# Two tiles in one product for q, k and up, and turned norms that pass DRAM block by block

## The chip, the cores and the metric

The kernel runs on one core of one Trainium2 chip. The metric is the device time of one execution in microseconds (us), the median of several runs. Everything is float32.

## The reference, cut to what matters

The input is 8 sequences of 2048 tokens with 256 features. A token passes an attention block and a feed-forward block, each behind a layer norm and followed by another one, with a residual sum:

```python
def layer(x):                                   # x: [8, 2048, 256]
    x = x + layernorm(attention(layernorm(x)))
    return x + layernorm(ffn(layernorm(x)))

def attention(h):                               # linear attention in chunks of 128 tokens
    q, k, v = h @ w_q.T, h @ w_k.T, h @ w_v.T
    sq, sk = elu(q) + 1, elu(k) + 1
    mem = (sq @ memory) / clip(sq @ memory_norm)
    A = (sq_chunk @ sk_chunk.T) * tril          # 128x128
    local = (A @ v_chunk + sq_chunk @ S) / clip(A.sum(-1) + sq_chunk @ z)
    S, z = S + sk_chunk.T @ v_chunk, z + sk_chunk.sum()
    return (g * mem + (1 - g) * local) @ w_o.T

def ffn(h):
    dense = silu(h @ W_up.T) @ W_down.T         # 256 -> 1024 -> 256
    # product-key routing: 4 heads, the best 8 of 1024 experts in each
    w = silu((h @ down_embed.T)[best] * softmax(scores[best]))
    return dense + sum(w * up_embed[best])
```

## The kernel before

A tile is one chunk of 128 tokens (tokens on the partitions, 256 features in a row). There are 128 tiles, taken so that the eight sequences alternate. Each engine's program is written out by hand as a loop over 142 steps: `pipeline(body)` calls `body(t, steady)`, and `t[n]` is the tile that stands at stage n in this step. In a given step `t[3]` is an early tile (its input is normed), `t[7]` is in the attention, `t[8]` has its second norm, `t[9]` and `t[10]` are in the routing and the up product, `t[12]` and `t[13]` in the two output products. All engines run free of each other and meet at semaphores alone, so the step of one engine is shifted against that of another.

**TensorE in one step**, in this order: up product of `t[10]` (L723 to L735, 16 products with 128 columns, the two halves into banks 1 and 2), q and k of `t[7]` (L752 to L756, 8 products with 128 columns), v, the expert output product of `t[13]`, the routing product of `t[9]`, the attention scores of `t[7]` (L791), the first half of the expert down product, the state and memory products, the product of masked scores and v (L817, it waits for the mask that VectorE applies at L1153), the second half of the down product, the state update (L835), the hidden output product of `t[12]` (L845). A float32 product is recorded as two weight loads and two matmuls of equal shape. All products made by `product` have line L691.

**The turned norms.** TensorE needs the two layer norms with features on the partitions: `xn1T` (first norm, used at stage 7) and `xn2T` (second norm, used by the routing and down products at stage 9 and by the up product at stage 10). They are not turned on TensorE except for the first three and the last tiles. VectorE transposes inside blocks of 32x32 (L1088, L1115) into `xn1_blocks` and `xn2_blocks`, SyncE (SP) stores the 128 KB to DRAM in one transfer of 1 KB rows (L448, L444), waits for it, and fetches it back rearranged with eight transfers of 16 KB in pieces of 128 bytes (`gather_chunks`, L437). `xn1T` and `xn2T` have two buffers each. In the step in which TensorE runs the routing product of `t[9]`, SP fetches the turned second norm of `t[8]`.

**SP's queue in one step**: store of the second norm (L444), store of the first norm (L448), store of the transposed expert weights `w_way` (512 KB, L452, it waits for VectorE's L1127), fetch of `xn2T`, store of the k features (L460), fetch of the expert weights (L430, four transfers), load of the next input (L469), fetch of the k features (L430, four), fetch of `xn1T`, store of the output (L483, it waits for VectorE's L1109). That is 30 transfers.

**GpSimd** adds the experts' weights of the heads with two accumulating transfers in each step: the pairs (1 MB, L597), then the sum of both (512 KB, L558). They run on the same 16 DMA engines as SP's transfers.

**ScalarE** takes q and k from PSUM (relu and exp, L975 and L977) and the hidden layer (silu, L947 and L892); **VectorE** makes the k and q features `sig` (L1078), the norms and the expert selection.

Of the kernel before, what the change touches and what calls it, by code (L numbers as in the profile page):

```python
# [6 lines left out]
def sandwich_kernel(nc, hidden, w_q, w_k, w_v, w_o, gate, memory, memory_norm,  # L7
# [52 lines left out]
    LATE = TILES - 2  # L60

# [7 lines left out]
    with ctx:  # L69
# [68 lines left out]
        xn1_way = nc.dram_tensor("xn1_way", [2, P, D], fp32).ap()  # L138
        xn2_blocks = sb("xn2_blocks", [P, D])
        xn2_way = nc.dram_tensor("xn2_way", [2, P, D], fp32).ap()  # L140
# [6 lines left out]
        hT = sb("hT", [P, 3, IC, P])  # L147
# [24 lines left out]
        eqk = bank[1].rearrange("p (c n) -> p c n", n=P)  # L172
# [13 lines left out]
        s_ue_cent = sem("up_embed_centred")  # L186
        s_last_ps = sem("last_weights_turned")
# [144 lines left out]

        def y_bank(t):
            return bank[{TILES - 3: 5, TILES - 2: 1, TILES - 1: 2}.get(t, 4)][:, 0:D]
# [61 lines left out]
        def _(sp):  # L396
# [36 lines left out]
            def gather_chunks(dst, way, s_in):  # L433

                for j in range(BLOCKS):
                    for c in range(DC):
                        sp.dma_start(dst[j * BLOCK:(j + 1) * BLOCK, c, :].rearrange("p (i t) -> p i t", t=BLOCK),  # L437
                                     way.rearrange("(i q) (j c t) -> j c q i t", q=BLOCK, j=BLOCKS, c=DC)[j, c]).then_inc(s_in, 16)

            def body(t, steady):  # L440
                if t[8] is not None:
                    if EARLY <= t[8] < LATE:
                        wait(sp, s_xn2_blocks_turned, t[8] + 1 - EARLY)
                        sp.dma_start(xn2_way[t[8] % 2, :, :], xn2_blocks[:, :]).then_inc(s_xn2_blocks_out[t[8] % 2], 16)  # L444
                if t[5] is not None:
                    if t[5] >= EARLY:
                        wait(sp, s_xn1_blocks_turned, t[5] + 1 - EARLY)
                        sp.dma_start(xn1_way[t[5] % 2, :, :], xn1_blocks[:, :]).then_inc(s_xn1_blocks_out[t[5] % 2], 16)  # L448
# [26 lines left out]
                if t[5] is not None:  # L475
                    if t[5] >= EARLY:
                        moved(sp, s_xn1_blocks_out, t[5], 1, TILES, EARLY)
# [768 lines left out]
```

## Time and profile before

| | us |
|---|---|
| median of 3 runs | 2849.07 (2846.18 to 2849.6) |
| the profiled execution | 2846.18 |
| span of its trace | 2844.4 |
| TensorE matmul busy | 2813.8, 99% |
| TensorE weight loads | 2268.5, 80% |
| VectorE, ScalarE, GpSimd busy | 2422.0, 2525.5, 2062.6 |
| DMA engines busy, mean of 16 | 78% |

Busy times are sums over the span, and engines work at the same time. The profiled execution was 2846.18 us, 1.8 us more than its span. Of TensorE's busy time, matmuls are pipelined and their ends are modelled, so the time that a group takes is best read from the start of the group to the start of the next one.

### The profile page before, as it was taken

Reading aid. Unit: us, or ns where it says so; the run is one execution under the profiler, and the core shown is the slowest. Engines: PE = TensorE matmul, PEld = TensorE weight load, DVE = VectorE, ACT = ScalarE, POOL = GpSimd, SP = SyncE. Lnnn points to the kernel's source line nnn. Section 1 sums busy time; section 2 is a strip of 40 time slices with the busy share of each in tenths; the row PEclk is TensorE's granted clock in tenths of the full one; section 3 lists DMA queues with packets and bytes.
Section 4 is the critical chain, followed back from the end, with each engine's and each line's share of the span. In section 5 each row is a group of like instructions: output and inputs, shape, how many; then the busy total and the mean of one; then the engine's idle time right before and its main releaser. Section 6 shows DMA issues by size and latency. Waiting matters only on the chain.

```text
span 2844.4 us, 49057 instructions
## 1 busy us (share of the span) xinstructions
PE 2813.8 (99%) x14724; PEld 2268.5 (80%) x14724; DVE 2422.0 (85%) x6125; ACT 2525.5 (89%) x3618; POOL 2062.6 (73%) x2460
## 2 busy tenths in 40 slices
PE   8899999999999999999999999999999999999999
PEld 6688788878878887888788878887887788788877
DVE  5888888888888888888888888888888888888876
ACT  5889998999898899989998999899889989998997
POOL 4677777777777777777777777777777777777774
PEclk9999999999999999999999999999999999999999
DMA  4788788778887887888778778877878888778774
GB/s 120 146 172 168 170 168 172 166 170 171 171 168 168 171 172 167 170 172 170 170 168 173 167 170 168 172 166 170 171 171 168 169 171 171 169 168 172 155 153 118
DMA packets 592909, 471.71 MB, mean 166 GB/s; under 512 B 377731, under 2 KB 527364, under 8 KB 592644
## 3 DMA queue, kind: packets, MB, share of 16 engines
q0 software_dynamic: 52832, 199.77, 40.0%
q1 hardware_dynamic: 539812, 268.81, 37.7%
q8 instruction: 117, 1.92, 0.3%
q14 instruction: 148, 1.21, 0.1%
HBM read 137.37 MB, written 131.20 MB: 94 GB/s over the span
## 4 chain that ended last, share of the span: by engine, by line
PE 94%; POOL 2%; ACT 1%; DVE 1%; issue 1%; DMA 0%; SPq 0%; POOLq 0%; DVEq 0%; ACTq 0%
PE banks L691 88%; PE banks L835 4%; PE banks L817 2%; POOL sums L539 1%; POOL rstd L525 0%; DMA wexp<-wexp 0%; POOL wexp L597 0%; ACT L1008 0%; DVE w_blocks L1127 0%; POOL cand_best L584 0%; ACT wexp L1008 0%; PE banks L626 0%; PE banks L648 0%; DVE picked L1074 0%; PE banks L668 0%
## 5 line engine op out<-in xcount | busy, mean ns | idle before, releaser
L539 POOL TENSOR_TENSOR sums<-scores 128x1024 f32<-128x1024 f32 x512 | 1005.7, 2049 | 73.9 <-ACT scores L1025 73.9
L525 POOL TENSOR_TENSOR rstd<-var_eps,minus_half 128x1 f32<-128x1 f32 x512 | 510.4, 997 | 42.0 <-ACT y_sq L935 15.5
L691 PE MATMUL banks<-deT,xn2T 128*128 128x512 f32 x1024 | 484.2, 596 | 2.5 <-DVE picked L1074 2.1
L691 PEld LDWEIGHTS banks<-xn2T,wupT 128*128 128x128 f32 x4096 | 477.2, 192 | 9.7 <-DVE state L1181 3.3
L691 PE MATMUL banks<-xn2T,wupT 128*128 128x128 f32 x4096 | 478.2, 275 | 2.5 <-DVE state L1181 2.5
L691 PE MATMUL banks<-ue,gT 128*128 128x256 f32 x2048 | 462.8, 379 | 0.0
L691 PE MATMUL banks<-wdownT,hT 128*128 128x256 f32 x2048 | 462.7, 379 | 0.0
L691 PEld LDWEIGHTS banks<-wdownT,hT 128*128 128x128 f32 x2048 | 389.1, 190 | 56.4 <-issue 2.6
L691 PEld LDWEIGHTS banks<-ue,gT 128*128 128x128 f32 x2048 | 388.8, 190 | 52.7
L577 POOL TENSOR_TENSOR wexp<-wexp,w_last 128x1 f32<-128x1 f32 x127 | 132.7, 1045 | 370.7 <-ACT z_last L1014 370.7
L691 PEld LDWEIGHTS banks<-deT,xn2T 128*128 128x128 f32 x1024 | 185.4, 191 | 135.8 <-issue 125.2
L553 POOL TENSOR_TENSOR cprob<-cmask,cdif 128x112 f32<-128x112 f32 x128 | 58.9, 460 | 271.1 <-DVE cmask L1208 271.1
L691 PE MATMUL banks<-route,xn2T 128*128 128x512 f32 x512 | 240.8, 592 | 0.8 <-ACT xn2T L882 0.8
L1074 DVE SCALAR_TENSOR_TENSOR picked<-sums,cand_best,banks 128x1024 f32<-128x1024 f32 x128 | 163.8, 1280 | 51.5 <-POOL sums L539 51.5
L1173 DVE SCALAR_TENSOR_TENSOR picked<-sums,cand_best,banks 128x1024 f32<-128x1024 f32 x128 | 163.9, 1280 | 46.3 <-PE banks L691 45.6
L1194 DVE SCALAR_TENSOR_TENSOR prob<-picked,rz,prob 128x1024 f32<-128x1024 f32 x128 | 166.2, 1298 | 36.9 <-ACT prob L939 35.4
L1082 DVE SCALAR_TENSOR_TENSOR prob<-picked,rz,prob 128x1024 f32<-128x1024 f32 x128 | 166.7, 1302 | 27.2 <-ACT prob L986 26.9
L947 ACT ACTIVATE hT<-banks 128x512 f32<-128x512 f32 x128 | 76.6, 598 | 125.2 <-PE banks L691 125.0
L1186 DVE SCALAR_TENSOR_TENSOR picked<-sums,cand_best,banks 128x1024 f32<-128x1024 f32 x128 | 163.3, 1276 | 11.6 <-POOL sums L539 11.4
L896 ACT ACTIVATE wexp<-prob 128x1024 f32<-128x1024 f32 x127 | 134.2, 1057 | 39.1 <-DVE w_blocks L1127 39.1
L961 ACT ACT_TABLE_LOAD x128 | 164.2, 1283 | 2.3
L947 ACT ACT_TABLE_LOAD x128 | 164.2, 1283 | 2.3
(162 smaller groups left out, 6649.3 us busy)
## 6 DMA issues: line engine op xcount, KB each, us to landing
wexp<-wexp POOLq DMA_DIRECT2D x127, 1024.0 KB, 8.4
wexp<-wexp POOLq DMA_DIRECT2D x127, 512.0 KB, 4.7
w_way<-w_blocks SPq DMA_DIRECT2D x127, 512.0 KB, 2.6
g_parts<-w_way SPq DMA_DIRECT2D x508, 128.0 KB, 5.6
xn_way<-xn_blocks SPq DMA_DIRECT2D x248, 128.0 KB, 1.8
x_in<-_attn_hidden_states_dram SPq DMA_DIRECT2D x128, 128.0 KB, 4.6
out_dram<-x_out SPq DMA_DIRECT2D x128, 128.0 KB, 1.8
xn1T<-xn_way SPq DMA_DIRECT2D x1000, 16.0 KB, 2.3
```

Source lines behind the costliest of these rows:

```text
L525: return nc.gpsimd.tensor_tensor(rstd[:, n, m:m + 1], var_eps[:, n, m:m + 1], minus_half[:, :], ALU.pow)
L539: return nc.gpsimd.tensor_tensor(sums[:, k, :, :], scores[:, k, 0:XIN].unsqueeze(2).broadcast_to([P, XIN, NKEYS]), scores[:, HEADS + k, :] ...
L577: nc.gpsimd.tensor_tensor(weights(t[9])[:, 0, LAST_IN:], weights(t[9])[:, 0, LAST_IN:], w_last[:, t[9] % 2:t[9] % 2 + 1], ALU.add).then_in ...
L691: last = nc.tensor.matmul(out, lhs(c), rhs(c), start=(start and c == 0), stop=(stop and c == chunks - 1))
L896: nc.scalar.activation(weights(t[10])[:, 3, :], prob[:, 3, :], ACT.Silu).then_inc(s_head_3_weights_ready, 1)
L947: nc.scalar.activation(flat(hT[:, t[9] % 3, 4:8, :]), u_ps[1][:, :], ACT.Silu).then_inc(s_hidden_1_ready, 1)
L961: nc.scalar.activation(prob[:, 3, :], head(sums, 3), ACT.Exp, bias=neg_max[:, t[9] % 2, 3:4]).then_inc(s_head_3_prob_ready, 1)
L1074: nc.vector.scalar_tensor_tensor(picked[:, 0, :], head(sums, 2), best[:, 2, TOP - 1:TOP], down, ALU.is_ge, ALU.mult).then_inc(s_head_2_sel ...
L1082: nc.vector.scalar_tensor_tensor(prob[:, 2, :], picked[:, 0, :], rz[:, t[10] % 2, 2:3], prob[:, 2, :], ALU.mult, ALU.mult).then_inc(s_head ...
L1173: nc.vector.scalar_tensor_tensor(picked[:, 0, :], head(sums, 0), best[:, 0, TOP - 1:TOP], down, ALU.is_ge, ALU.mult).then_inc(s_head_0_sel ...
L1186: nc.vector.scalar_tensor_tensor(picked[:, 1, :], head(sums, 1), best[:, 1, TOP - 1:TOP], down, ALU.is_ge, ALU.mult).then_inc(s_head_1_sel ...
L1194: nc.vector.scalar_tensor_tensor(prob[:, 1, :], picked[:, 1, :], rz[:, t[9] % 2, 1:2], prob[:, 1, :], ALU.mult, ALU.mult).then_inc(s_head_ ...
```

## The change

1. **q, k and up for two tiles at once.** From tile 12 on, q and k are made for two neighbouring tiles in one product with 256 columns: in an even step (`t[7]` even) k of tiles t and t+1, in an odd step q of tiles t+1 and t+2, always one matrix, 4 products, 512 columns of PSUM. The first q pair is made by itself in the step of tile 12, in bank 0. The up product of tiles 12 to 125 is treated the same way: the step of an even tile makes a half of the 1024 hidden units for both tiles, the next step the other half. `sig` gets a third buffer, `hT` a fourth. The up product of an even tile u now needs `xn2T` of tile u+1 at its start, and TensorE waits for it there.
2. **Turned norms.** `xn1T` and `xn2T` are laid out as [partition, chunk, tile, token] with four tiles, so that two neighbouring tiles are one row of 256. SP stores the blocks with four transfers of 32 KB in pieces of 128 bytes (`scatter`), each to its place in an already transposed array in DRAM, and fetches it back with one transfer of 128 KB in rows of 512 bytes (`turned_in`).
3. **The first norm two steps earlier.** At tiles 10 and 14 (`AHEAD`) one additional tile is normed and turned, so that from there on the input norm and `xn1T` are two stages earlier than before, since q of tile t+2 is needed in the step of tile t.

```diff
+    PAIRED = 12
+    AHEAD = (10, 14)
+    TURNED = 4
-        xn1T = sb("xn1T", [P, 2, DC, P])
-        xn2T = sb("xn2T", [P, 2, DC, P])
+        xn1T = sb("xn1T", [P, DC, TURNED, P])
+        xn2T = sb("xn2T", [P, DC, TURNED, P])
-        sig = sb("sig", [P, 2, 2 * DC, P])
+        sig = sb("sig", [P, 3, DC, 2, P])
-        xn2_way = nc.dram_tensor("xn2_way", [2, P, D], fp32).ap()
+        xn2_way = nc.dram_tensor("xn2_way", [2, D, P], fp32).ap()
...
+        def ahead(t, stage):
+
+            for lead in range(len(AHEAD) + 1):
+                u = t[stage - lead]
+                if u is not None and u not in AHEAD and len([a for a in AHEAD if a < u]) == lead:
+                    return u
+            return None
+
+        def hidden_at(t):
+            return t // 2 * 2 + 2 if paired_up(t) else t + 1
+
+        def paired_up(t):
+            return PAIRED <= t < LATE
...
+            def scatter(way, blocks, s_out):
+
+                for i in range(BLOCKS):
+                    sp.dma_start(way.rearrange("(k q) t -> q k t", q=BLOCK)[:, :, i * BLOCK:(i + 1) * BLOCK],
+                                 blocks[i * BLOCK:(i + 1) * BLOCK, :].rearrange("q (k t) -> q k t", t=BLOCK)).then_inc(s_out, 16)
+
+            def turned_in(dst, way, s_in):
+                sp.dma_start(dst, way.rearrange("(c p) n -> p c n", p=P)).then_inc(s_in, 16)
...
                     if EARLY <= t[8] < LATE:
                         wait(sp, s_xn2_blocks_turned, t[8] + 1 - EARLY)
-                        sp.dma_start(xn2_way[t[8] % 2, :, :], xn2_blocks[:, :]).then_inc(s_xn2_blocks_out[t[8] % 2], 16)
-                if t[5] is not None:
-                    if t[5] >= EARLY:
-                        wait(sp, s_xn1_blocks_turned, t[5] + 1 - EARLY)
-                        sp.dma_start(xn1_way[t[5] % 2, :, :], xn1_blocks[:, :]).then_inc(s_xn1_blocks_out[t[5] % 2], 16)
+                        scatter(xn2_way[t[8] % 2, :, :], xn2_blocks, s_xn2_blocks_out[t[8] % 2])
+                x = ahead(t, 5)
+                if x is not None:
+                    if x >= EARLY:
+                        xn1_out(x)
...
-                        moved(sp, s_xn2_blocks_out, t[8], 1, LATE, EARLY)
-                        gather_chunks(xn2T[:, t[8] % 2, :, :], xn2_way[t[8] % 2, :, :], s_xn2_blocks_in[t[8] % 2])
+                        moved(sp, s_xn2_blocks_out, t[8], BLOCKS, LATE, EARLY)
+                        wait(sp, s_up_0_in_psum, t[8] - 2)
+                        turned_in(xn2T[:, :, t[8] % TURNED, :], xn2_way[t[8] % 2, :, :], s_xn2_blocks_in[t[8] % 2])
...
+            def up(t, half):
+
+                if not paired_up(t):
...
+                else:
+                    first = t // 2 * 2 % TURNED
+                    for k in range(2):
+                        ic = 4 * (t % 2) + 2 * half + k
+                        last = product(two_tiles(u_ps[half])[:, k, :, :], DC, lambda c: wupT[:, c, ic * P:(ic + 1) * P],
+                                       lambda c: xn2T[:, c, first:first + 2, :])
+                return last
+
+            def two_tile_q_or_k(dst, w, t):
+                for ec in range(DC):
+                    last = product(two_tiles(dst)[:, ec, :, :], DC, lambda c: w[:, c, ec * P:(ec + 1) * P],
+                                   lambda c: xn1T[:, c, t % TURNED:t % TURNED + 2, :])
+                return last
...
+                    if paired_up(u) and u % 2 == 0:
+                        moved(pe, s_xn2_blocks_in, u + 1, 1, LATE, EARLY)
+                    wait(pe, s_state_ready, u + 2, KEPT)
+                    wait(pe, s_hidden_1_ready, u)
+                    up(u, 1).then_inc(s_up_1_in_psum, 1)
+                    wait(pe, s_hidden_0_ready, u)
+                    up(u, 0).then_inc(s_up_0_in_psum, 1)
...
+                    elif t[7] % 2 == 0:
+                        two_tile_q_or_k(qk_ps, wkT, t[7]).then_inc(s_qk_in_psum, 1)
+                    elif t[7] < TILES - 1:
+                        two_tile_q_or_k(qk_ps, wqT, t[7] + 1).then_inc(s_qk_in_psum, 1)
...
+                for lead, a in enumerate(AHEAD):
+                    if t[3 - lead] == a:
+                        if a - 1 <= EARLY:
+                            dve.wait_ge(s_early_ps, TURN['xn1', a - 2] + 1)
+                        dve.wait_ge(s_x_rstd, a)
+                        xn1_made(a - 1)
+                        dve.wait_ge(s_xn1_ready, a)
+                    if t[4 - lead] == a:
+                        xn1_turned(a)
```

## Rows read from the trace of the kernel before

**Rows 1.** The page, part 1: busy us, share of the span, instructions.

```profile
PE 2813.8 (99%) x14724; PEld 2268.5 (80%) x14724; DVE 2422.0 (85%) x6125; ACT 2525.5 (89%) x3618; POOL 2062.6 (73%) x2460
```

**Rows 2.** The page, part 4: the chain that ended last, shares by engine.

```profile
PE 94%; POOL 2%; ACT 1%; DVE 1%; issue 1%; DMA 0%; SPq 0%; POOLq 0%; DVEq 0%; ACTq 0%
```

**Rows 3.** Timeline of TensorE, one step: start, us, line, op, out<-in, shape, count.

```profile
1503.58 1.88 PE L691 MATMUL banks<-route,xn2T 128*128 128x512 f32 x4
...
1509.21 0.60 PE L817 MATMUL banks<-v_one,at 128*128 128x258 f32 x2
...
1512.23 3.62 PE L691 MATMUL banks<-wdownT,hT 128*128 128x256 f32 x16
1515.68 3.73 PE L691 MATMUL banks<-xn2T,wupT 128*128 128x128 f32 x32
1519.25 1.06 PE L691 MATMUL banks<-xn1T,wqT 128*128 128x128 f32 x8
...
1521.04 1.03 PE L691 MATMUL banks<-wvo,xn1T 128*128 128x256 f32 x4
...
1525.36 1.02 PE L691 MATMUL banks<-route,xn2T 128*128 128x512 f32 x2
```

**Rows 4.** Waits of TensorE: waited for, us in total, times, longest us.

```profile
PE banks L817 <- DVE at L1153: 9.2, 5, 3.5
```

**Rows 5.** Timeline of VectorE, same step; idle before and releaser in brackets.

```profile
1499.64 1.28 DVE L1074 SCALAR_TENSOR_TENSOR picked<-sums,cand_best,banks 128x1024 f32<-128x1024 f32 x1 [0.38 <-POOL sums L539]
...
1501.76 1.28 DVE L1082 SCALAR_TENSOR_TENSOR prob<-picked,rz,prob 128x1024 f32<-128x1024 f32 x1 [0.24 <-ACT prob L986]
...
1504.34 0.44 DVE L1115 STREAM_TRANSPOSE xn_blocks<-xn 128x256 f32<-128x256 f32 x1
...
1508.24 0.41 DVE L1144 BATCH_NORM_STATS2 stats<-x_in 128x6 f32<-128x256 f32 x1
...
1508.62 0.28 DVE L1153 TENSOR_TENSOR at<-banks,causal 128x128 f32<-128x128 f32 x1
1509.91 0.16 DVE L1156 TENSOR_SCALAR dens<-banks 128x2 f32<-128x2 f32 x1 [1.01 <-PE banks L817]
```

**Rows 6.** Timeline of ScalarE, same step.

```profile
1499.46 0.60 ACT L975 ACTIVATE rqk<-banks 128x512 f32<-128x512 f32 x1 [0.51 <-PE banks L691]
```

**Rows 7.** Timeline of SP's queue: start, us to issue, line, transfer, count.

```profile
1504.68 0.43 SPq L483 DMA_DIRECT2D out_dram<-x_out  x1
1505.16 0.43 SPq L444 DMA_DIRECT2D xn_way<-xn_blocks  x1
...
1507.12 0.32 SPq L452 DMA_DIRECT2D w_way<-w_blocks  x1
1507.49 4.13 SPq L437 DMA_DIRECT2D xn2T<-xn_way  x8
...
1517.60 0.74 SPq L469 DMA_DIRECT2D x_in<-_attn_hidden_states_dram  x1
```

**Rows 8.** Timeline of SP's queue at the start, a load of 256 rows.

```profile
1.71 0.43 SPq L401 DMA_DIRECT2D sums<-in_L_attn_w_q_dram  x1
```

**Rows 9.** Timeline of GpSimd, same step: the accumulating transfer of the pairs.

```profile
1510.06 1.25 POOL L597 DMA_DIRECT2D wexp<-wexp  x1
```

**Rows 10.** Line L437, transfers issued between 1507 and 1508.5 us.

```profile
L437 SPq DMA_DIRECT2D xn2T<-xn_way x2: 433/604/775, 1507.5 to 1508.0; - x2
DMA to landing us min/median/max: 2.3/2.4/2.5
```

**Rows 11.** Line L437, transfers issued between 1511 and 1511.66 us.

```profile
L437 SPq DMA_DIRECT2D xn2T<-xn_way x2: 432/432/432, 1510.7 to 1511.2; - x2
DMA to landing us min/median/max: 1.7/4.6/7.5
```

**Rows 12.** The page, part 6: transfers, KB each, median us to landing.

```profile
xn_way<-xn_blocks SPq DMA_DIRECT2D x248, 128.0 KB, 1.8
x_in<-_attn_hidden_states_dram SPq DMA_DIRECT2D x128, 128.0 KB, 4.6
```

More of the change, by code:

```diff
@@ new lines, in up @@
+            def up(t, half):
+                if not paired_up(t):
+                    for k in range(4):
+                        ic = 4 * half + k
+                        last = product(u_ps[half][:, k * P:(k + 1) * P], DC, lambda c: wupT[:, c, ic * P:(ic + 1) * P],
+                                       lambda c: xn2T[:, c, t % TURNED, :])
+                else:
[5 more added lines that the diff above has]
+                return last
@@ L718, in body @@
                         turn_wdown(0, 0)
-                    if t[10] == TILES - 3:
+                    if u == TILES - 3:
                         turn_xn('xn2', xn2, s_xn2_ready, LATE)
-                    if t[10] == TILES - 2:
+                    if u == TILES - 2:
                         turn_xn('xn2', xn2, s_xn2_ready, LATE + 1)
-                    wait(pe, s_state_ready, t[10] + 2, KEPT)
-                    for k in range(4):
-                        ic = 4 + k
-                        last = product(u_ps[1][:, k * P:(k + 1) * P], DC, lambda c: wupT[:, c, ic * P:(ic + 1) * P],
-                                       lambda c: xn2T[:, t[10] % 2, c, :])
@@ L728, in body @@
-                    last.then_inc(s_up_1_in_psum, 1)
-                    if not steady:
-                        wait(pe, s_hidden_0_ready, t[10])
-                    for k in range(4):
-                        ic = k
-                        last = product(u_ps[0][:, k * P:(k + 1) * P], DC, lambda c: wupT[:, c, ic * P:(ic + 1) * P],
-                                       lambda c: xn2T[:, t[10] % 2, c, :])
-                    last.then_inc(s_up_0_in_psum, 1)
+                    if paired_up(u) and u % 2 == 0:
+                        moved(pe, s_xn2_blocks_in, u + 1, 1, LATE, EARLY)
@@ L831, in body @@
                     if not steady:
-                        wait(pe, s_hidden_0_ready, t[8] - 1)
+                        wait(pe, s_hidden_0_ready, up_done(t[8] + 8), TILES)
                     if t[8] < KEPT:
@@ L1174, in body @@
                                                    ALU.is_ge, ALU.mult).then_inc(s_head_0_selected, 1)
-                if t[3] is not None:
-                    dve.wait_ge(s_x_stats, t[3] + 1)
-                    nc.vector.bn_aggr(mv[:, LN_X, t[3] % 2, :], stats[:, LN_X, t[3] % 2, :]).then_inc(s_x_moments, 1)
+                x = ahead(t, 3)
+                if x is not None and x - 1 not in AHEAD:
+                    x_moments(x)
                 if t[8] is not None:
@@ L1195, in body @@
                                                    ALU.mult, ALU.mult).then_inc(s_head_1_weighed, 1)
+                for lead, a in enumerate(AHEAD):
[7 more added lines that the diff above has]
+                        xn1_turned(a)
+                x = ahead(t, 3)
+                if x is not None and x - 1 in AHEAD:
+                    x_moments(x)
                 if t[7] is not None:
```

273 lines of the change are left out of this document (178 added, 95 removed).

## The prediction

> **What bounds the kernel now.** I read the page first: TensorE is busy for 99% of the span while no other engine is over 89% [rows 1], and the chain of work that ended last runs over TensorE for 94% of the span [rows 2]. Then the timeline of TensorE in one step in the middle [rows 3]: no row carries an idle time, and from the routing product of one step (1503.58) to that of the next (1525.36) there are 21.78 us. 128 such steps are 2788 us of the span of 2844.4; the other 56 us are set-up, filling and draining. TensorE's largest wait for anybody is 9.2 us in 5 places, for the mask at L1153 [rows 4]. So the middle is a pure stream of products, and an edit is worth what it takes out of that stream, as long as nobody who feeds TensorE becomes late.
>
> **Part 1, the products.** The next starts in rows 3 give the price of each shape. Sixteen instructions with 256 columns (hidden output) last from 1512.23 to 1515.68, 3.45 us, 215.6 ns each. Thirty-two with 128 columns (up) last from 1515.68 to 1519.25, 3.57 us, 111.6 ns each; the sixteen of q and k from 1519.25 to 1521.04, 1.79 us, 111.9 ns each. The change turns every two of 128 columns into one of 256. Per step 48 instructions, 5.36 us, become 24 of 215.6 ns, 5.17 us: 0.19 us less. The columns stay the same, only what an instruction costs beside its columns goes, so this is small: 3.5% of the two groups. Count: up 114 tiles x 16 = 1824 new instructions; k and q 58 pairs x 16 = 928 (the first q pair in bank 0 is among them, moved and not added); together 2752, each 223.3 - 215.6 = 7.7 ns cheaper than the two it replaces. **Sum: -21.2 us.** Bounds: the other instructions near 256 columns (L817 and its neighbours, 258 columns) follow each other in the same manner [rows 3], so I see no reason for more than 1 ns either way, 3 us in all.
>
> A rule of the Trainium skill puts this part lower. In "TensorE: Matmul & The Clock Gate", section "Wait — 56ns, not 53.3ns?", a matmul has a fixed cost of about 2.5 ns beside its columns. By that one instruction less saves 2.5 ns and the part is 2752 x 2.5 = 6.9 us; the rows show 7.7 ns, and I go by the rows.
>
> **What covers it.** The saving holds only if the others keep pace with a step of 21.59 us. VectorE: the mask ends at 1508.90 and TensorE's L817 needs it at 1509.21 [rows 3, 5], 0.31 us of slack, and this is the tightest feeder. Going back from there VectorE works without a pause to L1082, which waits 0.24 us for ScalarE [rows 5]; ScalarE in turn waits 0.51 us at L975 for the end of q and k [rows 6]. That chain starts from TensorE behind the shortened groups, so it comes earlier by the same 0.19 us. The chain that does not start there comes over GpSimd's sums into L1074 [rows 5]; it has the 0.31 and the 0.24 us, less a few hundredths for semaphores, against 0.19 needed. VectorE also waits 1.01 us for L817 in each step [rows 5]. ScalarE's and VectorE's operations keep their number and size, as q alone or k alone of two tiles is 512 columns again. Cost: nothing. Without this cover each step would lose up to 0.19 us and the part would be gone. The new waits for the hidden layer and its fourth buffer ask for things that are done a step before; nothing.
>
> **Part 2, the turned norms.** SP issues 8 stores and 2 fetches in place of 2 and 16, 22 transfers a step in place of 30, so its queue is shorter by 8 x 0.48 = 3.8 us (0.48 from L483 to L444 [rows 7]). That by itself is worth nothing, TensorE never waits for SP. What matters is that an even step's up product now needs the second norm of tile u+1 at its own start, 1515.68, where before the routing product needed it at 1525.36 [rows 3]: 9.7 us less. Before, the last piece was issued at 1511.2 and landed 7.5 us later [rows 11], at 1518.7: **under the old scheme this wait would fail by 3 us.** So the new order in SP's queue decides. VectorE has turned the norm at 1504.78 [rows 5], SP stores the output at 1504.68 and is free at 1505.16. Four stores of the second norm and four of the first, 0.48 us each, end at 1509.0; then `w_way` (it was issued at 1507.12, so 1.9 us later than before [rows 7]); then the fetch at about 1509.4. The four stores of the second norm are issued by 1507.1 and land in about 1.8 us [rows 12], at 1508.9: not late for the fetch. Behind `w_way` a fetch landed in 2.3 to 2.5 us [rows 10], so this one lands at about 1511.9, 3.8 us ahead of the up product. An issue costs 0.43 us for 256 rows too [rows 8], so I take 0.48 for the stores with 256 pieces. The edge is the pairs' accumulating transfer, issued at 1510.06 [rows 9]: of the two fetches issued at 1510.7 and 1511.2 one landed in 1.7 and one in 7.5 us [rows 11], so its data fill the engines from some 1.2 to 1.7 us after its issue, 1511.3 to 1511.8. The new fetch has its data out at about 1511.5. It is close, but a fetch cut off by half still has until 1515.68. Cost taken: nothing; bounds: 0 and the rival below. The first norm's fetch at the end of SP's step is needed two steps later as before, nothing.
>
> **Part 3, the earlier first norm.** The input is needed one step after its load: issued at 1517.60 [rows 7], landing in 4.6 us [rows 12], read at 1508.24 + 21.78 = 1530.0 [rows 5], so 7 us of slack; nothing. At the two places where a tile is slipped in, VectorE has five more operations of 0.16 to 0.44 us [rows 5], 0.8 to 2.2 us against a slack of 0.31: 0 to 1.9 us each, I take 1 us each. At the end TensorE makes the last tile's q and k, 1.79 us [rows 3], a step or two earlier; where it then waits for VectorE, that is not collected: 0 to 1.8, I take 1 us. **Sum: +3 us.**
>
> **The sum.** 2846.2 - 21.2 + 3 = 2828.0 us for an execution like the profiled one. It was 2.9 us under the median of the runs, so 2831 against 2849.07. By the bounds 2825 to 2836.
>
> **Rivals.**
> - *Late fetch, slower.* If the data of the fetch come behind those of the accumulating transfer, it lands as in rows 11: 7.5 us after 1509.4, 1516.9, up to 1518.7 where the late one landed. TensorE then stands for 1.2 to 3.0 us at L691's up product in every even step, 57 times, 68 to 171 us, middle 120: 2951. It decides from the point where eight stores take over 0.55 us each, or land after more than 3 us, or hold up the `w_way` data behind them in the same queue by 0.6 us. For it: no row shows a store of 128-byte pieces, and 512 KB of `w_way` now lie right before the fetch. Against it: the fetches in such pieces landed in 1.7 us when nothing else ran [rows 11]. Chance 0.23. The Trainium skill speaks for this rival: "DMA: Bandwidth & Descriptors", section "Specifications", says that below 512 B an engine reads, modifies and writes. No run so far shows it; if a piece cost twice as much the queue would be behind by about that much.
> - *The gain is eaten, no change.* The fetch is late by 0.4 us on average: 57 x 0.35 = 20 us, 2851. Or a 256-column instruction in these places saves only 2.5 ns (223.3 - 2.5 = 220.8 ns): 6.9 - 3 us, 2845. Chance 0.12 for both.
> - *The seams cost nothing and more is collected at the ends:* under 2825, chance 0.03. That the pairing is not done at all is excluded by the diff.
>
> **How the numbers follow.** A measurement of this kernel can tell about 0.2% from no change, that is below 2843.4 and above 2854.8. The forecast has 0.62. Faster: 0.62 + 0.03 = 0.65; same 0.12; slower 0.23. The range starts at 2823; up to 2836 it holds about 0.63, with the no-change cases 0.75, and it reaches to 2880 to take in a fetch that is late by less than 0.9 us in the even steps, which brings it to 0.8.
>
> **What would show it.** Right: up groups of 16 instructions with 256 columns and 3.45 us, a step of 21.59 us, no idle ahead of them, and the fetch of `xn2T` landing in 2 to 3 us. Wrong: idle time of TensorE ahead of the up product in every second step, put down to a transfer; mask waits of L817 in every step (then VectorE's slack was less than 0.19 us); SP's `w_way` issued after 1509.5 by this step's clock; or an up group of 3.53 us. Waits at L817 in two steps near tiles 10 and 14 would be the seams.

## The result and the profile after

The changed kernel takes 2836.33 us (median of 6 runs, 2832.46 to 2838.54); the kernel before, on the same chip, takes 2849.34 us (6 runs, 2846.18 to 2851.68). The ratio is 0.9952, with a 95% interval of 0.9941 to 0.9962: faster by 13 us. The profiled execution took 2835.43 us, its span is 2833.7 us in place of 2844.4, so 10.7 us less.

The page of the changed kernel, parts 1 and 4, then the stores of the turned norms from part 6 (out<-in, queue, count, KB each, us from issue to landing):

```profile
PE 2797.6 (99%) x11972; PEld 2176.6 (77%) x11972; DVE 2423.5 (86%) x6125; ACT 2525.7 (89%) x3618; POOL 2053.0 (72%) x2460
...
PE 85%; POOL 6%; ACT 3%; DVE 3%; issue 2%; SPq 1%; DMA 1%; DVEq 0%; POOLq 0%; ACTq 0%
...
xn_way<-xn_blocks SPq DMA_DIRECT2D x992, 32.0 KB, 1.7
```

TensorE runs 2752 products less than in [rows 1], and is still busy for 99% of the span; every other engine has the work it had. The chain of work leans on TensorE for 85% in place of the 94% of [rows 2]: the others have come nearer.

The timeline of TensorE in one step of the changed kernel, to be laid beside [rows 3]:

```profile
1501.76 1.88 PE L749 MATMUL banks<-route,xn2T 128*128 128x512 f32 x4
...
1507.39 0.60 PE L908 MATMUL banks<-v_one,at 128*128 128x258 f32 x2
...
1510.41 3.62 PE L749 MATMUL banks<-wdownT,hT 128*128 128x256 f32 x16
1513.86 3.62 PE L749 MATMUL banks<-xn2T,wupT 128*128 128x256 f32 x16
1517.32 1.89 PE L749 MATMUL banks<-xn1T,wkT 128*128 128x256 f32 x8
1519.04 1.03 PE L749 MATMUL banks<-wvo,xn1T 128*128 128x256 f32 x4
...
1523.36 1.88 PE L749 MATMUL banks<-route,xn2T 128*128 128x512 f32 x4
```

From routing product to routing product there are 21.60 us, before 21.78. The up group lasts from 1513.86 to 1517.32, 3.46 us (before 3.57); k or q from 1517.32 to 1519.04, 1.72 us (before 1.79). No row has an idle time.

**Where the 10.7 us are.** I split the span at two events that both kernels have, the starts of the 13th and of the 120th tile's routing product. The timeline of TensorE of the kernel before has them in these rows:

```profile
305.57 1.88 PE L691 MATMUL banks<-route,xn2T 128*128 128x512 f32 x4
...
2636.28 1.88 PE L691 MATMUL banks<-route,xn2T 128*128 128x512 f32 x4
```

and that of the changed kernel in these:

```profile
313.18 1.88 PE L749 MATMUL banks<-route,xn2T 128*128 128x512 f32 x4
...
2625.74 1.88 PE L749 MATMUL banks<-route,xn2T 128*128 128x512 f32 x4
```

The 107 steps between them went from 2330.7 to 2312.6 us: -18.1. The part before them became longer by 7.6 us (1.7 of it is the first q pair, which is made there ahead of its time). The part behind them went from 208.1 to 207.9 us, -0.2. Together -10.7. So the stream of products gave most of what was forecast, and the start and the end took back more than forecast. This sum is good to a few us only: in the profiled executions the first routing product starts anywhere from 39.6 to 43.6 us, and in two executions of one and the same kernel (experiments 4 and 5, two block buffers) at 39.90 and at 43.16.

The waits of TensorE (waited for, us in total, times, longest):

```profile
PE banks L908 <- DVE at L1293: 14.2, 10, 3.4
```

In [rows 4] the same wait had 9.2 us in 5 places. Three of the new ones are in the steps around the slipped tiles (1.44, 0.27 and 1.99 us), where one that was there (1.24) has become longer (1.63) and one of 0.15 is gone. Two are single steps of the middle (0.30 us at 945.64 and 0.32 at 1788.60), and one is at the end (0.44).

### The profile page after: what moved, and what is told of

It is laid out like the page before. It is cut to its first block, busy times and chain, and to the rows that moved or that the text cites. A ratio compares the mean times of both kernels' runs of the same rounds, so it can differ in the third digit from the quotient of the medians.

```text
span 2833.7 us, 43226 instructions
## 1 busy us (share of the span) xinstructions
PE 2797.6 (99%) x11972; PEld 2176.6 (77%) x11972; DVE 2423.5 (86%) x6125; ACT 2525.7 (89%) x3618; POOL 2053.0 (72%) x2460
## 4 chain that ended last, share of the span: by engine, by line
PE 85%; POOL 6%; ACT 3%; DVE 3%; issue 2%; SPq 1%; DMA 1%; DVEq 0%; POOLq 0%; ACTq 0%
PE banks L749 79%; PE banks L926 3%; POOL sums L593 3%; PE banks L908 2%; POOL rstd L579 1%; POOL wexp L655 1%; ACT L1112 1%; SPq L470 0%; ACT wexp L1112 0%; POOL cand_best L638 0%; SPq L476 0%; DMA xn_way<-xn_blocks 0%; DVE picked L1201 0%; DVE prob L1259 0%; DVE w_blocks L1267 0%
## 5 line engine op out<-in xcount | busy, mean ns | idle before, releaser
L749 PE MATMUL banks<-xn2T,wupT 128*128 128x256 f32 (+1 forms) x2272 | 464.8, 359 | 2.5 <-DVE state L1321 2.5
L749 PEld LDWEIGHTS banks<-xn2T,wupT 128*128 128x128 f32 x2272 | 398.5, 190 | 51.0 <-DVE state L1321 3.3
L631 POOL TENSOR_TENSOR wexp<-wexp,w_last 128x1 f32<-128x1 f32 x127 | 125.6, 989 | 353.2 <-ACT z_last L1118 353.2
L988 ACT ACTIVATE hT<-banks 128x512 f32<-128x512 f32 x228 | 136.8, 600 | 74.5 <-PE banks L749 74.0
```

The costliest lines, as they stand in the source:

```text
L631: nc.gpsimd.tensor_tensor(weights(t[9])[:, 0, LAST_IN:], weights(t[9])[:, 0, LAST_IN:], w_last[:, t[9] % 2:t[9] % 2 + 1], ALU.add).then_in ...
L749: last = nc.tensor.matmul(out, lhs(c), rhs(c), start=(start and c == 0), stop=(stop and c == chunks - 1))
L988: nc.scalar.activation(hT[:, pair_of(t):pair_of(t) + 2, ic:ic + 2, :].rearrange("p t i n -> p i t n"), two_tiles(u_ps[half]), ACT.Silu).th ...
```

## The experiments

All ratios are against the kernel before on the same chip, with 95% intervals. A step is the time between the starts of two routing products of TensorE. The account to be tested: the gain is that of the products alone, 7.7 ns for each, the new transfers only make the pairs possible, and the slipping in of two tiles takes some of it back. Its rivals: the transfers carry the gain themselves; the pairs would be in time with the old transfers too; the 7.7 ns are a fixed cost of an instruction.

**1. The transfers alone.** The new stores, the single fetch and the buffers stay; nothing is paired and no tile is slipped in.

```
-    PAIRED = 12
-    AHEAD = (10, 14)
+    PAIRED = TILES
+    AHEAD = ()
+    UP_PAIRED = TILES
...
-            return PAIRED <= t < LATE
+            return UP_PAIRED <= t < LATE
```

> The new way of the turned norms alone (four stores of 128-byte pieces, one fetch, four buffers), with q, k and up made tile by tile as before and no tile slipped in. Theory A, the gain is the price of an instruction: the step of TensorE stays at 21.78 us and the time at 2849 us (ratio 1.000, within 0.1%). Rival B, the gain comes from the shorter transfer queue (22 transfers a step in place of 30): a step of 21.60 us as in the changed kernel, 2829 us.

Measured: 2847.89 us, ratio 0.9997 (0.9987 to 1.0006). The timeline of its TensorE:

```profile
1504.41 1.88 PE L750 MATMUL banks<-route,xn2T 128*128 128x512 f32 x4
...
1516.51 3.73 PE L750 MATMUL banks<-xn2T,wupT 128*128 128x128 f32 x32
...
1526.18 1.88 PE L750 MATMUL banks<-route,xn2T 128*128 128x512 f32 x4
```

The step is 21.77 us with the groups of 128 columns, as before. By themselves the eight fewer transfers a step are worth nothing that can be measured. They are not without effect on the other transfers: the four fetches of the expert weights (`g_parts`) land in 7.5 us at the median, before 5.6, the input in 5.7, before 4.6, the pairs' accumulating transfer in 9.7, before 8.4, and it is the same in the changed kernel (7.4, 5.6, 9.7). TensorE doesn't wait for any of these. Whether the stores in small pieces or the larger fetches do this, no run separates.

**2. Only the up product in pairs.** As experiment 1, with `UP_PAIRED = 12`: q and k for one tile, nothing slipped in.

> Only the up product for two tiles, q and k tile by tile, no tile slipped in, new transfers. Theory A: 1824 instructions of 256 columns for 3648 of 128, 7.7 ns each, 14 us: a step of 21.65 us, 2835 us in all, ratio 0.995. This would be no slower than the whole change (2836.3), since the two places where a tile is slipped in cost about what q and k gain. Rival: the whole change gains from q and k too, after the two places: then this is slower than it by 5 us or more, 2841 us.

Measured: 2835.77 us, ratio 0.9955 (0.9940 to 0.9970). Its TensorE:

```profile
1499.63 1.88 PE L750 MATMUL banks<-route,xn2T 128*128 128x512 f32 x4
...
1511.73 3.62 PE L750 MATMUL banks<-xn2T,wupT 128*128 128x256 f32 x16
1515.18 1.05 PE L750 MATMUL banks<-xn1T,wkT 128*128 128x128 f32 x8
...
1521.29 1.88 PE L750 MATMUL banks<-route,xn2T 128*128 128x512 f32 x4
```

The step is 21.66 us: 0.12 less, which is 16 x 7.7 ns. This part alone is as fast as the whole change, so what q and k in pairs give is lost again somewhere.

**3. Only q and k in pairs.**

```
         def paired_up(t):
-            return PAIRED <= t < LATE
+            return False
```

> Only q and k for two tiles, with the two tiles slipped in; up tile by tile. Theory A: a step of 21.71 us (928 instructions x 7.7 ns = 7 us less), and 6 to 7 us lost in the steps around tiles 10 and 14, so 2849 us, ratio 1.000. Rival: the places cost 2 us as forecast, 2844 us, ratio 0.998.

Measured: 2849.41 us, ratio 1.0002 (0.9992 to 1.0011). The steps are 21.71 to 21.72 us, 0.06 less (8 x 7.7 ns), and the 107 middle steps together are 6.1 us shorter. Against it stand the steps around the slipped tiles, from the sixth on 22.78, 23.44, 21.78, 22.28 and 25.78 us. Gain and loss cancel within the interval; the loss belongs to the slipping in and not to the up product.

**4. Two block buffers for the first norm.** In the seams VectorE waits in front of L1182, as these rows of the changed kernel's VectorE show (idle us before it and what ended it in brackets):

```profile
175.91 0.45 DVE L1182 STREAM_TRANSPOSE xn_blocks<-xn 128x256 f32<-128x256 f32 x1 [1.68 <-DMA xn_way<-xn_blocks]
...
244.07 0.45 DVE L1182 STREAM_TRANSPOSE xn_blocks<-xn 128x256 f32<-128x256 f32 x1 [2.33 <-DMA xn_way<-xn_blocks]
```

`xn1_blocks` is one buffer. VectorE turned the first slipped tile at 165.95, but SP came to its stores only behind the fetches of the expert weights, the input, the k features and `xn1T`:

```profile
169.92 1.89 SPq L476 DMA_DIRECT2D xn_way<-xn_blocks  x4
```

The next tile's turning has to wait until these stores have read the buffer. With a second buffer that wait has nothing to ask for:

```
-        xn1_blocks = sb("xn1_blocks", [P, D])
+        xn1_blocks = sb("xn1_blocks", [P, 2, D])
...
-                scatter(xn1_way[x % 2, :, :], xn1_blocks, s_xn1_blocks_out[x % 2])
+                scatter(xn1_way[x % 2, :, :], xn1_blocks[:, x % 2, :], s_xn1_blocks_out[x % 2])
...
-                moved(dve, s_xn1_blocks_out, x - 1, BLOCKS, TILES, EARLY)
-                nc.vector.transpose(turned_chunks(xn1_blocks), blocks(xn1[:, :])).then_inc(s_xn1_blocks_turned, 1)
+                moved(dve, s_xn1_blocks_out, x - 2, BLOCKS, TILES, EARLY)
+                nc.vector.transpose(turned_chunks(xn1_blocks[:, x % 2, :]), blocks(xn1[:, :])).then_inc(s_xn1_blocks_turned, 1)
```

> The whole change, but the transposed blocks of the first norm have two buffers, so that VectorE need not wait for the stores of the slipped-in tile before it turns the next one. Theory A: these two waits (1.7 and 2.3 us of VectorE in the changed kernel's trace) are what stops TensorE at the mask, 1.4 and 2.0 us: both go, 3 to 4 us less than the changed kernel, 2833 us, ratio 0.994. Rival: the added operations of VectorE stop TensorE anyway, and only the place of the wait moves: 2836 us, ratio 0.9955.

Measured: 2831.59 us, ratio 0.9938 (0.9923 to 0.9953). Its VectorE at the first slipped tile, in the timeline:

```profile
174.36 0.44 DVE L1182 STREAM_TRANSPOSE xn_blocks<-xn 128x256 f32<-128x256 f32 x1
```

The idle time is gone, there and at the second slipped tile (240.19). Of the steps of the changed kernel, 23.45 became 21.78 and 27.47 became 23.44: 1.67 and 4.03 us. The second number is larger than the wait, and the timeline of TensorE says why. The changed kernel:

```profile
247.04 1.14 PE L749 MATMUL banks<-mem_x,sig 128*128 128x258 f32 x4
250.16 0.81 PE L908 MATMUL banks<-v_one,at 128*128 128x258 f32 x2 [1.99 <-DVE at L1293]
250.77 3.48 PE L749 MATMUL banks<-deT,xn2T 128*128 128x512 f32 x4
254.09 1.03 PE L926 MATMUL banks<-v_one,sk_nat 128*128 128x258 f32 x4
```

and with two buffers:

```profile
245.57 1.03 PE L749 MATMUL banks<-mem_x,sig 128*128 128x258 f32 x4
246.44 0.60 PE L908 MATMUL banks<-v_one,at 128*128 128x258 f32 x2
246.88 1.88 PE L749 MATMUL banks<-deT,xn2T 128*128 128x512 f32 x4
248.59 1.03 PE L926 MATMUL banks<-v_one,sk_nat 128*128 128x258 f32 x4
```

From `mem_x` to L908 there are 2.25 us more (3.12 against 0.87), then 0.17 more to `deT`, and the four `deT` products take 3.32 in place of 1.71 us: 1.61 more. Together 4.03. Behind the idle time TensorE ran at about half its speed. So some 1.7 of the 4.03 us are clock. The granted clock in the stretch from 240 to 262 is 0.92 for the changed kernel, as its window view shows, and 1.00 with two buffers:

```profile
240.00:262.00 22.00, 20.01 (x91) 14.50 (x90) 16.25 (x45) 16.48 (x25) 11.49 (x17) 0.92 0.75 154
```

(window: length, busy time and count of TensorE, its weight loads, VectorE, ScalarE and GpSimd, granted clock, DMA share, GB/s.)

The clock is not lost each time. Experiment 3 has the same wait of 1.99 us at the same place, and its timeline goes on at full speed:

```profile
253.25 0.67 PE L908 MATMUL banks<-v_one,at 128*128 128x258 f32 x2 [1.99 <-DVE at L1293]
253.76 1.88 PE L749 MATMUL banks<-deT,xn2T 128*128 128x512 f32 x4
255.48 1.03 PE L926 MATMUL banks<-v_one,sk_nat 128*128 128x258 f32 x4
```

The granted clock from 240 to 262 is 1.00 there, and the step 25.78 us, only 2.3 above the 23.44. Experiment 7, which has the changed kernel's single buffer too, has 25.73; the second execution of the changed kernel (experiment 5) has 27.44. So the single buffer costs 2.3 us at the second seam in every execution and 1.7 more in some.

**5. The changed kernel and two buffers once more, side by side.** The same two kernels, since the difference is small.

> The changed kernel once more, on the chip and beside the runs of the next two: ratio 0.9952 as before, 2836 us. It is what the next two are held against.

> The changed kernel with two block buffers for the first norm, again. Theory A: the 4.0 us by which its steps at the two places were shorter are a real gain, so 4 to 5 us under the changed kernel of this call (ratio to before 0.994). Rival: the difference of the medians was one of chips, and they are equal here.

Measured: 2837.28 us, ratio 0.9961 (0.9948 to 0.9975), and 2832.11 us, ratio 0.9938 (0.9925 to 0.9950). The second buffer gives 5.2 us, against 1.67 + 4.03 = 5.7 from the steps. The kernel with it is faster than the kernel before and than the changed one. The traces alone would say more, 6.5 us from span to span in experiment 4, but 1.2 of that are behind the last routing product. There all kernels have a wait of 2.1 to 2.2 us for VectorE, and behind it the eight `deT` products took 5.40 us in the changed kernel and 3.70 in the two executions with two buffers, by the clock again: experiment 7 has 3.70 with one buffer.

**6. The old store and the old pieces for the second norm.** This asks whether the new transfers are needed for the pairs.

```
-                        scatter(xn2_way[t[8] % 2, :, :], xn2_blocks, s_xn2_blocks_out[t[8] % 2])
+                        sp.dma_start(xn2_way[t[8] % 2, :, :], xn2_blocks[:, :]).then_inc(s_xn2_blocks_out[t[8] % 2], 16)
...
-                        turned_in(xn2T[:, :, t[8] % TURNED, :], xn2_way[t[8] % 2, :, :], s_xn2_blocks_in[t[8] % 2])
+                        gather_chunks(xn2T[:, :, t[8] % TURNED, :], xn2_way[t[8] % 2, :, :], s_xn2_blocks_in[t[8] % 2])
```

> The whole change, but the second norm goes its old way: one store of 1 KB rows and eight fetches of 16 KB. Theory A, said in the prediction: the last fetch is issued about 6.4 us after the norm is turned, lands 7.5 us later behind the accumulating transfer of the pairs, and the up product of the even steps stands for about 3 us: 57 x 3 = 171 us more than the changed kernel, 3007 us, ratio 1.055, with idle time of TensorE ahead of up in every second step. Rival B: the transfers have room (the step is rearranged since), and this costs nothing: 2836 us. The new way of storing would then be needed for nothing but the layout.

Measured: 3119.2 us, ratio 1.0956 (1.0924 to 1.0988). TensorE's wait for the fetch (total, times, longest), and two up groups of its timeline:

```profile
PE banks L756 <- DMA xn2T<-xn_way: 167.8, 57, 4.3
```

```profile
1439.29 5.37 PE L756 MATMUL banks<-xn2T,wupT 128*128 128x256 f32 x16 [2.77 <-DMA xn2T<-xn_way]
...
1487.91 6.64 PE L756 MATMUL banks<-xn2T,wupT 128*128 128x256 f32 x16 [3.52 <-DMA xn2T<-xn_way]
```

57 waits of 2.94 us on average: the mechanism of the rival, at the length that the prediction gave. The order of the transfers is the one it named, too: ahead of the first of these two groups, six of the eight fetches land in 1.7 to 2.4 us, and the last two, issued 1.2 and 1.7 us behind the pairs' accumulating transfer, in 7.2 and 7.0. The time lost is 283 us against the changed kernel, though, not 171. The up group that follows a wait takes 5.1 to 6.7 us in place of 3.6, in all 57 places. The same window view for the second group above and for an up group without a wait, at 1462.63:

```profile
1487.90:1494.40 6.50, 6.49 (x17) 5.24 (x18) 2.93 (x5) 2.64 (x3) 4.28 (x6) 0.54 0.73 151
...
1462.63:1466.09 3.46, 3.46 (x18) 3.04 (x17) 3.46 (x7) 2.44 (x3) 0.73 (x3) 1.00 1.03 221
```

Behind the idle time the granted clock is 0.54 (near 1.2 GHz of 2.4), in the group without a wait it is 1.00. The 57 steps with a wait take 26.50 us on average, 4.9 more than the 21.60 of the others. Of this 2.94 are the wait, and the other 2.0 for the most part the slow group behind it (5.4 in place of 3.6 us).

**7. The fetch one place later.** The store `sk_way` goes ahead of the fetch of the second norm.

```
+                if t[7] is not None:
+                    if EARLY <= t[7] < KEPT:
+                        wait(sp, s_sk_blocks_turned, t[7] + 1 - EARLY, KEPT - EARLY)
+                        sp.dma_start(sk_way[t[7] % 2, :, :], sk_blocks[:, :]).then_inc(s_sk_blocks_out[t[7] % 2], 16)
                 if t[8] is not None:
...
-                if t[7] is not None:
-                    if EARLY <= t[7] < KEPT:
-                        wait(sp, s_sk_blocks_turned, t[7] + 1 - EARLY, KEPT - EARLY)
-                        sp.dma_start(sk_way[t[7] % 2, :, :], sk_blocks[:, :]).then_inc(s_sk_blocks_out[t[7] % 2], 16)
```

> The whole change, but SP fetches the second norm behind the store of the k features, 0.5 to 2 us later than now. Theory A, the edge forecast in the prediction: the fetch now lands 2.9 to 4.4 us after its issue, 2 us ahead of the up product; issued later its data meet those of the accumulating transfer and it lands after 6 to 8 us: 0.5 to 3 us of idle time in the even steps, 30 to 170 us, 2865 to 3005 us. Rival B: the 2 us in hand take it up, 2836 us.

Measured: 2843.77 us (8 runs, 2836.72 to 2858.56), ratio 0.9988 (0.9968 to 1.0007). In its profiled execution (2855.28 us) the waits, and one of the late groups:

```profile
PE banks L749 <- DMA xn2T<-xn_way: 11.4, 3, 4.2
```

```profile
1630.30 5.41 PE L749 MATMUL banks<-xn2T,wupT 128*128 128x256 f32 x16 [4.17 <-DMA xn2T<-xn_way]
```

Three of the 57 fetches were late. The landing took 2.7 us at the median and 9.5 at the longest. Two of the three were issued about 0.6 us behind the pairs' accumulating transfer, later against it than any other fetch. But fetches issued 0.3 to 0.5 us behind it landed in 2.8 to 3.1 us, and the third late one was issued together with it, as more than half of all were, the rest of these in time. So the edge is real and lies just behind the place that the fetch has in the changed kernel, but it is no line that all cross at once, and what decides for the single fetch stays open. Neither theory had that.

**8. The fetch earlier.** Two buffers, and SP's four stores of the first norm behind the fetch of the second.

```
-                if x is not None:
-                    if x >= EARLY:
-                        xn1_out(x)
                 if t[11] is not None:
...
                         turned_in(xn2T[:, :, t[8] % TURNED, :], xn2_way[t[8] % 2, :, :], s_xn2_blocks_in[t[8] % 2])
+                if x is not None:
+                    if x >= EARLY:
+                        xn1_out(x)
```

> Two block buffers, and SP fetches the second norm before it stores the first one, about 2 us earlier. Theory A: in the changed kernel the fetch is on time in nearly every even step, so more room brings nothing that can be measured: within 1 us of the kernel with two block buffers, the landing 2 to 3 us after the issue in place of up to 4.4. Rival: single late fetches cost some runs several us, and with more room the median falls by 2 us or more and the runs spread less.

Measured: 2832.28 us, ratio 0.9943 (0.9931 to 0.9956), the same as two buffers alone on that chip (2832.11, experiment 5). The fetches now land in 2.4 us at the median and 3.5 at most, but nobody waits for them in either order.

**9. The up product in 64 columns.** The kernel before, with each product of up cut in two, asks where the 7.7 ns come from.

```
-                        last = product(u_ps[1][:, k * P:(k + 1) * P], DC, lambda c: wupT[:, c, ic * P:(ic + 1) * P],
-                                       lambda c: xn2T[:, t[10] % 2, c, :])
+                        for h in range(2):
+                            last = product(u_ps[1][:, k * P + h * 64:k * P + (h + 1) * 64], DC, lambda c: wupT[:, c, ic * P:(ic + 1) * P],
+                                           lambda c: xn2T[:, t[10] % 2, c, h * 64:(h + 1) * 64])
```

> The kernel before with every up product cut once more, into 64 columns: 64 instructions a step in place of 32. Theory A, an instruction costs a fixed 5 ns beside its columns: 64 x (53.3 + 5) = 3.73 us for 3.57, a step of 21.94 us, 2870 us. Rival B: the weight load, which each instruction has, sets a floor of some 107 to 112 ns, and 128 columns sit right on it: 64 x 110 = 7.0 us, a step of 25.2 us, about 3290 us, ratio 1.155.

Measured: 3306.34 us, ratio 1.1613 (1.1579 to 1.1647), a step of 25.35 us. Its TensorE:

```profile
1506.10 7.25 PE L691 MATMUL banks<-xn2T,wupT 128*128 128x64 f32 x64
1513.19 1.11 PE L691 MATMUL banks<-xn1T,wqT 128*128 128x128 f32 x8
```

7.09 us for 64 instructions, 110.8 ns each: with half the columns an instruction takes what it takes with 128. So there is a floor of some 111 ns that doesn't depend on the moving columns, 128-column instructions lie on it, and the 215.6 ns of 256 columns are above it. It is not the whole of the saving. By the mean distance of the starts within the groups of the trace before (600 to 2500 us), an instruction takes 111.6 ns with 128 columns, 215.8 with 256 and about 429.4 with 512. Twice 215.8 less 429.4 is 2.2 ns that an instruction costs beside its columns. On the line through 256 and 512 columns, 128 would take 109.0 ns (an estimate), and they take 2.6 more. So of the 7.4 ns that these means give for a merge (2 x 111.6 - 215.8), about two thirds are the floor, twice 2.6, and one third is the fixed cost of one instruction. What is common to 64 and 128 columns is the 128 x 128 weight load. That it is the load that sets the floor is argued and not shown, as no run here changes its size. The Trainium skill, in "TensorE: Matmul & The Clock Gate", section "LDWEIGHTS (loading the stationary operand)", gives a load as its columns divided by 1.2, in ns. For 128 columns that makes 107 ns, an estimate from the page; the 110.8 ns here are near it.

**10. What bounds next.** The changed kernel leaves out half of the hidden layer's output product (its chunks 4 to 7, tiles 0 to 126), so that TensorE has less to do.

```
-                        product(y_bank(t[12]), IC, lambda c: hT[:, t[12] % 4, c, :], lambda c: wdownT[:, c, :], stop=False).then_inc(s_y_hidden_in_psum, 1)
+                        product(y_bank(t[12]), IC // 2, lambda c: hT[:, t[12] % 4, c, :], lambda c: wdownT[:, c, :], stop=False).then_inc(s_y_hidden_in_psum, 1)
```

> The changed kernel with half of the hidden output product left out (4 of 8 chunks, tiles 0 to 126), 1.73 us less of TensorE in each step, so its output is not the reference's. It asks how much shorter the step may get before another engine sets it. Theory A: the chain from L908 over VectorE, GpSimd's sums and back to the mask has about 0.2 to 0.4 us left, so the step stops at 21.2 to 21.4 us and TensorE waits some 1.4 us at L908 in each: about 2795 us. Rival B: the others follow by the full 1.73 us: a step of 19.87 us, 2617 us.

Measured: 2809.63 us, ratio 0.9868 (0.9840 to 0.9897). Its waits and its L908:

```profile
PE banks L908 <- DVE at L1293: 151.9, 123, 3.8
```

```profile
1517.04 0.67 PE L908 MATMUL banks<-v_one,at 128*128 128x258 f32 x2 [1.24 <-DVE at L1293]
```

1.73 us of products are gone from each step, and most steps fall by only some 0.24, to 21.34 to 21.38: TensorE now waits for the mask in nearly every step. The chain that ended last, by engine, no longer leans on TensorE:

```profile
POOL 43%; DVE 35%; issue 11%; PE 4%; ACT 3%; DMA 2%; SPq 1%; DVEq 0%; POOLq 0%; ACTq 0%
```

What bounds this kernel is the loop over GpSimd (its sums above all) and VectorE, and it is about 0.2 us shorter than the changed kernel's step. A further saving on TensorE gives nothing past that.

## Why the prediction held, point by point

The forecast was 2831 us, the kernel takes 2836.33, at the upper edge of the 2825 to 2836 that the sum's own bounds gave: 13 us were gained where 18 were forecast. The sign and the step were right, the terms of the start and the end were too small, and of the mechanism one sentence was wrong: it is not only what an instruction costs beside its columns that goes.

**The products** held. Forecast: 24 instructions of 215.6 ns, up in 3.45 us, a step of 21.59. Measured: 3.46 us and 21.60. Experiments 2 and 3 separate its shares, 0.12 and 0.06 us a step, as 16 and 8 times 7.7 ns. Over the 107 middle steps the saving is 18.1 us, against 107 x 24 x 7.7 ns = 19.8 by the forecast. Of the missing 1.7, 0.8 is the price itself (7.4 ns by the means of experiment 9, in place of 7.7), and 0.8 lies in single slow steps: four of 22.14, 21.79, 22.15 and 21.85 us, where before there were two, of 22.13 and 22.15. The price was read from rows, so it came out right although the reason given for it did not: "only what an instruction costs beside its columns goes" is a third of it, and two thirds are the floor under 128 columns, which the prediction didn't see (experiment 9). By the Trainium skill's 2.5 ns, "TensorE: Matmul & The Clock Gate", section "Wait — 56ns, not 53.3ns?", the whole part would have been 6.9 us. The trace has such a cost, 2.2 ns, but it does not agree that this is all that a merge saves, because of the floor.

**The cover** held. VectorE's mask in the changed kernel, ahead of L908 at 1507.39:

```profile
1506.80 0.28 DVE L1293 TENSOR_TENSOR at<-banks,causal 128x128 f32<-128x128 f32 x1
```

It ends at 1507.08, 0.31 us ahead, as in [rows 3, 5]. The chain that comes from TensorE moved up with it, as argued. Experiment 10 says how much more there was: about 0.2 us. The cover fails in single steps, as the waits of 0.30 and 0.32 us in the middle show.

**The transfers** held on their order, less on their margin. SP's queue in that step:

```profile
1503.02 3.92 SPq L476 DMA_DIRECT2D xn_way<-xn_blocks  x8
1506.99 0.46 SPq L504 DMA_DIRECT2D w_way<-w_blocks  x1
1507.55 0.38 SPq L480 DMA_DIRECT2D xn2T<-xn_way  x1
```

Moved by the 1.82 us between the two routing products (1503.58 and 1501.76), `w_way` is at 1508.81 where the forecast said 1509.0, and the fetch at 1509.37 where it said 1509.4. The stores land in 1.7 us, forecast 1.8. But the fetch landed in 4.4 us, not in 2.3 to 2.5. The view of tile `xn2T` (all 123 fetches: duration of the issue in ns, first and last start; landing in us):

```profile
L480 SPq DMA_DIRECT2D xn2T<-xn_way x123: 382/382/390, 92.0 to 2734.5; - x123
...
DMA to landing us min/median/max: 2.3/2.9/4.4
```

1507.55 + 4.4 = 1511.95, which is 1.9 us ahead of the up product at 1513.86; the forecast had 3.8. 4.4 is also the longest of all 123, their median is 2.9, so none is late. This margin is why they cost nothing; one issue later it is gone for some of them (experiment 7).

**The late fetch**, the rival of 0.23, did not come, because the stores were as quick as taken. Its own argument, that the old scheme would fail by 3 us, was right (2.94 in experiment 6). Its price was wrong: 68 to 171 us were worked out as waiting time alone, and 283 were measured, as each wait also takes the clock. The rule of the Trainium skill behind it, "DMA: Bandwidth & Descriptors", section "Specifications", would slow pieces under 512 B; the 992 stores of 128-byte pieces with their 1.7 us show nothing of it. They are too short to exclude it, as a landing is nearly as long with 128 KB (1.8 us), and other transfers do land later since (experiment 1).

**The seams** are the term that was mis-sized. Forecast: 2 us for both. Measured, against the steps of before: +0.39, +1.67, 0, +0.51 and +5.69, of the last 1.7 is the first q pair; 6.6 us in all. 0.5 us come back ahead of them and 0.1 behind them, so 5.9 us at the first mark. The prediction counted VectorE's five more operations. What two buffers leave is 0.39 + 0.51 = 0.9 us, inside its 0 to 1.9 each (in experiment 1, with the new transfers alone, the first of these steps takes 21.69 us; against that it is 1.08). What it left out is that the slipped tile is one more user of the single block buffer, whose stores SP issues late: a wait of VectorE for a transfer (experiment 4), 1.67 us at one seam and 2.3 at the other, there with another 1.7 of clock in this execution. The prediction named the added waits of TensorE and SP and what they ask for; VectorE's at L1182 it did not name.

**The end** was too small as well. Eight more shortened steps (-1.4) and the q made ahead (-1.7) should have given -3.1 there, -0.2 came: 2.9 us lost, forecast 1. Three waits are there that the kernel before does not have (TensorE):

```profile
2754.12 1.14 PE L749 MATMUL banks<-mem_x,sig 128*128 128x258 f32 x4 [0.26 <-ACT hT L988]
2755.70 0.67 PE L908 MATMUL banks<-v_one,at 128*128 128x258 f32 x2 [0.44 <-DVE at L1293]
...
2774.41 3.69 PE L749 MATMUL banks<-wdownT,hT 128*128 128x256 f32 x16 [0.60 <-ACT hT L988]
```

They hold 1.3 us, but cost 2.0: the two steps that they are in are 1.20 and 0.83 us longer than the same steps of before less their saving. Two steps ahead of them take 20.93 and 21.09 in place of 20.72 us, 0.6 more, with L908 late by too little to be shown as a wait. Another 0.2 is no loss, as the last two steps have fewer pairs than -1.4 supposes, and 0.1 is behind the last routing product. Two of the three waits are for the hidden layer (`hT`), and the prediction had put the new waits for it at nothing. No run here tests the end by itself. In the traces of experiments 2 and 3 the last eight steps gave what they should with up alone in pairs (0.8 us), and fell short by 1.3 with q and k alone.

Set against the forecast of -18.2 for an execution like the profiled one: the start +3.9 (7.6 - 1.7 - 2), the end +1.9 (2.9 - 1), the middle +1.7 (19.8 - 18.1), and that is the -10.7 of the spans. The medians are 13 us apart.

## What to carry to other kernels

A merge of small products pays by what the trace's next starts say of the two shapes, and here for the most part because the small one lay on a floor; read that price from rows, and then count as a term of its own every buffer that an extra iteration passes through, with the wait for its last reader. Work slipped in once can eat the gain of a hundred steps if it puts one more user on a single buffer; a second buffer (1 KB for each partition) returned 5 us. An idle time of TensorE is to be priced with the slow products that may follow it; behind the 57 waits of about 3 us in experiment 6 they cost another 2 each.

## What the runs showed of the hardware that was not expected

- Idle times of 1.99 us (changed kernel, L908), 2.77 and 3.52 us (experiment 6) are followed by products at down to half speed: `deT` in 3.32 in place of 1.71 us, an up group of 16 in 5.4 and 6.6 in place of 3.6, with a granted clock of 0.54 in the last. The length of the idle time alone does not decide this. The same 1.99 us at L908 are followed by full speed in experiments 3 and 7, and 3.44 us ahead of the same product in experiment 1 by a granted clock of 1.00 (116.5 to 122), while the 3.45 us at the same place of the kernel before are followed by 0.70 (113.3 to 119). Behind the waits of 1.63 and 1.44 us at L908 in the changed kernel nothing is slow: those steps are only 0.99 and 1.67 us longer than 21.78.
- A float32 instruction with 64 moving columns takes 110.8 ns, with 128 columns 111.6, with 256 columns 215.8, with 512 about 429.4.
- Stores of 32 KB in pieces of 128 bytes land in 1.7 us, no more than the 1.8 us of 128 KB in rows of 1 KB.
- A fetch of 128 KB with 512-byte pieces that is issued 0.5 us ahead of the pairs' accumulating transfer takes up to 4.4 us, one that is issued a place later, at about the same time as it, up to 9.5 us, with the median almost the same (2.9 and 2.7 us).
